# A router's products in four quarters of a bank, and three of eight tiles normalised on VectorE

## The reference, cut to what matters

```
xn = layernorm(x)                      # mean and variance over 256
scores = (xn @ router_w.T + router_b) / max(temperature, 0.1)     # 8192 x 8
gates = sinkhorn(scores)               # 3 rounds of logsumexp, then top 2
s = attention(xn);  ffn = xn + experts(xn, top 2)
out = x + s * silu(ffn)
```

## Time and profile before

| | |
|---|---|
| median of three runs | 1550.58 us |
| the profiled execution | 1555.48 us, span 1553.7 us |
| TensorE busy | 1497.1 us, 96% of the span |
| TensorE idle before L1109 for ScalarE's L864, first 140 us | 11.5 us in 4 waits |
| ScalarE idle before L852 for TensorE's L1109, first 140 us | 10.4 us in 20 waits |
| granted clock, 30 to 36.8 us | 0.50 |

### The profile page before, as it was taken

The page is one execution under the profiler, slowest core; times in us unless marked ns, Lnnn a source line. Parts: engine busy times, 40 slices in busy tenths (PEclk is TensorE's granted clock), DMA queues, the critical chain, the costliest instruction groups (busy, mean ns, idle before and its releaser), DMA issues.

```text
span 1553.7 us, 31511 instructions
## 1 busy us (share of the span) xinstructions
PE 1497.1 (96%) x11036; PEld 1175.4 (76%) x11036; DVE 916.5 (59%) x1730; ACT 788.9 (51%) x1269; POOL 750.6 (48%) x881
## 2 busy tenths in 40 slices
PE   5999799989999999999999999999999999999997
PEld 2546665758888888888888888788887878778775
DVE  7567889954444444444444444466765666576567
ACT  4767334413333333333333333566767776676674
POOL 4504188913666665444444444235365364734365
PEclk9999999989999999999999999999999999999999
DMA  9946432266474746242422351233576555556654
GB/s 324 392 162 216 173 137 72 75 215 228 158 247 158 242 156 241 75 165 77 157 76 89 133 213 56 92 135 123 189 244 218 181 188 179 187 193 202 218 178 136
DMA packets 181330, 267.93 MB, mean 172 GB/s; under 512 B 15944, under 2 KB 123264, under 8 KB 180800
## 3 DMA queue, kind: packets, MB, share of 16 engines
q1 hardware_dynamic: 149920, 196.79, 37.1%
q0 software_dynamic: 12960, 35.41, 6.9%
q10 hardware_dynamic: 18304, 33.72, 6.1%
HBM read 157.97 MB, written 107.89 MB: 171 GB/s over the span
## 4 chain that ended last, share of the span: by engine, by line
PE 83%; DVE 7%; ACT 4%; DMA 3%; issue 2%; SPq 1%; ACTq 0%; DVEq 0%
PE ps L1377 24%; PE ps L1300 18%; PE ps L1396 12%; PE ps L1319 8%; PE ps L1242 5%; PE ps L1386 4%; PE ps L1315 2%; PE ps L1359 2%; ACT WM L964 2%; PE ps L1191 2%; PE ps L1263 2%; PE ps L1119 1%; DMA u_d<-UN 1%; PE ps L1109 1%; DVE UN L1462 1%
## 5 line engine op out<-in xcount | busy, mean ns | idle before, releaser
L1377 PE MATMUL ps<-WR,FR 128*128 x1620 | 405.6, 400 | 1.9 <-DMA WR<-w_d 1.9
L1377 PEld LDWEIGHTS ps<-WR,FR 128*128 128x128 f32 x1620 | 296.2, 190 | 57.0 <-issue 2.1
L775 POOL DMA_INDIRECT y_d<-AUX x135 | 133.6, 990 | 297.0 <-DVE AUX L1943 295.5
L964 ACT ACTIVATE WM<-ps,bcs,trig 128x512 f32<-128x512 f32 x256 | 242.2, 1014 | 63.7 <-PE ps L1300 59.6
L1960 DVE TENSOR_TENSOR AUX<-AUX,ps 128x512 f32<-128x512 f32 x135 | 92.9, 688 | 304.7 <-ACT AUX L1011 304.7
L1011 ACT ACTIVATE AUX<-ps 128x512 f32<-128x512 f32 x135 | 80.6, 597 | 291.2 <-PE ps L1377 291.2
L1870 DVE TENSOR_SCALAR WM<-ps,vec,trig 128x512 f32<-128x512 f32 x208 | 196.6, 1031 | 46.8 <-ACT WM L964 46.6
L1300 PE MATMUL ps<-XH,WH 128*128 128x512 f32 x512 | 208.1, 407 | 7.8 <-issue 4.0
L1396 PE MATMUL ps<-WR,ABR 128*128 x540 | 207.1, 418 | 0.0
L1300 PE MATMUL ps<-XH,WL 128*128 128x512 f32 x512 | 200.6, 392 | 0.0
L1300 PE MATMUL ps<-XL,WH 128*128 128x512 f32 x512 | 200.6, 392 | 0.0
(11 more groups left out here) (268 smaller groups left out, 2497.7 us busy)
## 6 DMA issues: line engine op xcount, KB each, us to landing
US<-u_d SPq DMA_DIRECT2D x62, 512.0 KB, 4.7
u_d<-UN SPq DMA_DIRECT2D x120, 256.0 KB, 2.4
WR<-w_d SPq DMA_DIRECT2D x96, 256.0 KB
AUX<-y_d SPq DMA_DIRECT2D x32, 512.0 KB, 6.4
w_d<-WR ACTq DMA_DIRECT2D x24, 512.0 KB, 3.4
WM<-in_L_attn_x_dram SPq DMA_DIRECT2D x16, 512.0 KB, 9.6
xn_d<-WM SPq DMA_DIRECT2D x32, 256.0 KB, 6.2
mhl_d<-UNR ACTq DMA_DIRECT2D x16, 512.0 KB, 3.1
```

Of the source, the lines that this page charges most:

```text
L775: e.indirect_dma_start(y_d, bass.IndirectOffsetOnAxis(toks[:, n:n + 1], 0), YS[n % 4], None).then_inc(s_y[n % 4], 16)
L964: e.activation(rotated(q, 2 * x, i), b, ACT.Identity, bias=bcs[:, x, 0, i:i + 1], scale=trig[:, 0, i:i + 1]).then_inc(s_ca, 1)
L1377: mm = e.matmul(b[:, :], x, WR[:, bass.ds(off[m] + (2048 * z + 1024 * a + 512 * k), 512)], start=(k == 0 and x is xh and z == 0), stop=(k ...
```

## The change

The products of four pairs now follow each other as one block of eight, first the four with k = 0 into the four quarters, then the four with k = 1. The block of foursome g is issued after the transposes of pair 4g + 5 (the last one at the end). ScalarE's copies go to six buffers instead of two; four of these share their space with `XH` and `XL`, so ScalarE's first copy to `XH` waits for the last block. Tiles 1, 3 and 7 of each eight are normalised on VectorE instead of 3 and 7.

```
-        RT = AB
+        RT = [AB[:, 0, :], AB[:, 1, :], RTX[:, 0, :], RTX[:, 1, :], RTX[:, 2, :], RTX[:, 3, :]]
...
+        ON_DVE = (1, 3, 7)
...
             def routed(i):
                 e.wait_ge(s_rt, i + 1)
-                if i >= 2:
-                    e.wait_ge(s_rm, i - 1)
-                e.activation(RT[:, i % 2, 0:512], (bT, bH)[i % 2][:, :], ACT.Copy).then_inc(s_rtc, 1)
+                if i >= 6:
+                    e.wait_ge(s_rm, 4 * ((i - 6) // 4 + 1))
+                e.activation(RT[i % 6], (bT, bH)[i % 2][:, :], ACT.Copy).then_inc(s_rtc, 1)
...
-                for n in (2 * i, 2 * i + 1)[:2 - i % 2]:
-                    e.activation(X[:, n, :], X[:, n, :], ACT.Identity, bias=nmr[:, n:n + 1],
-                                 scale=rstd[:, n:n + 1]).then_inc(s_xn, 1)
+                for n in (2 * i, 2 * i + 1):
+                    if n % 8 not in ON_DVE:
+                        e.activation(X[:, n, :], X[:, n, :], ACT.Identity, bias=nmr[:, n:n + 1],
+                                     scale=rstd[:, n:n + 1]).then_inc(s_xn, 1)
...
+                else:
+                    e.wait_ge(s_rm, NT // 2)
                 e.activation(XH[:, k, :], pXT[:, :], ACT.Copy).then_inc(s_xtc, 1)
...
-            def rmm(i):
-                e.wait_ge(s_rtc, i + 1)
-                g, a = i // 4, 32 * (i % 4)
-                if a == 0 and g >= 4:
+            def rmm(g):
+                e.wait_ge(s_rtc, 4 * g + 4)
+                if g >= 4:
                     e.wait_ge(s_re, g - 3)
                 for k in range(2):
-                    mm = e.matmul(ps[g % 4][a:a + 32, 0:256], rwT[:, k, :], RT[:, i % 2, 256 * k:256 * k + 256],
-                                  start=(k == 0), stop=(k == 1))
-                mm.then_inc(s_rm, 1)
+                    for a in range(4):
+                        mm = e.matmul(ps[g % 4][32 * a:32 * a + 32, 0:256], rwT[:, k, :],
+                                      RT[(4 * g + a) % 6][:, 256 * k:256 * k + 256], start=(k == 0), stop=(k == 1))
+                mm.then_inc(s_rm, 4)
...
-            for i in range(NT // 2 + 1):
-                if i < NT // 2:
-                    rt(i)
-                if i == 1:
+            for i in range(NT // 2):
+                rt(i)
+                if i == 5:
                     e.wait_ge(s_rwl, 2)
-                if i >= 1:
-                    rmm(i - 1)
+                if i >= 5 and i % 4 == 1:
+                    rmm(i // 4 - 1)
                 if i >= 10 and i % 4 == 2:
                     back(i // 4 - 2)
+            rmm(7)
...
-                for n in range(a + 3, b, 4):
+                for n in (n for n in range(a, b) if n % 8 in ON_DVE):
```

More of the change, by code:

```diff
@@ L88, in program @@
         XB = sb("XB", [128, 4, D])
-        XH = sb("XH", [128, 2, 512], F32R)
-        XL = sb("XL", [128, 2, 512], F32R)
+        with nc.sbuf_tensor("XHL", [128, 4, 512], F32R) as XHL:
+            pass
+        RTX = sb("RTX", [128, 4, 512])
+        XH, XL = XHL[:, 0:2, :], XHL[:, 2:4, :]
         with nc.sbuf_tensor("XHJ", [128, 2, 4, 128], F32R) as XHJ:
@@ L312, in program, with on_act @@
                     firsts.setdefault(slots[k - 3], []).append(j // 4)
+        ON_DVE = (1, 3, 7)
+        def on_act(n):
+            return sum(i % 8 not in ON_DVE for i in range(n))
         host = {QE + 1 + 2 * k: k for k in range(QE)}
@@ L443, in _ @@
                 if q < NQ:
-                    e.wait_ge(s_xn, 3 * q + 3)
-                    e.wait_ge(s_xv, q + 1)
+                    e.wait_ge(s_xn, on_act(4 * q + 4))
+                    e.wait_ge(s_xv, 4 * q + 4 - on_act(4 * q + 4))
                     for a in range(2):
@@ L1103, in rt @@
                     e.wait_ge(s_rtc, i - 1)
-                e.wait_ge(s_xn, 2 * i + 2 - (i + 1) // 2)
-                if i % 2:
-                    e.wait_ge(s_xv, (i + 1) // 2)
+                e.wait_ge(s_xn, on_act(2 * i + 2))
+                if 2 * i + 2 > on_act(2 * i + 2):
+                    e.wait_ge(s_xv, 2 * i + 2 - on_act(2 * i + 2))
                 for n in range(2):
```

## The result

| | median, us | times | ratio to before, 95% interval |
|---|---|---|---|
| before | 1554.15 (1549.31 to 1560.92) | 20 | |
| changed | 1549.51 (1544.45 to 1555.44) | 20 | 0.9968 [0.9955, 0.998] |

The change makes the kernel 0.32% faster, 0.20 to 0.45%. In time that is 4.6 us where 7.5 were forecast. The time, 1549.51, lies outside the range of 1540.5 to 1548.5. One part of this needs no explanation by the kernel: the median of before, over 20 times, is 3.6 above the 1550.58 of the three shown, from which the forecast was subtracted. Taken from 1554.15 the forecast would be 1546.6, and the range 1544.1 to 1552.1, which holds the time measured. So the range was missed by the number that the forecast started from; the gain itself is 2.9 smaller than forecast, and by the interval of the ratio it is 3.1 to 7.0 us.

What follows compares the result with a forecast made beforehand. TensorE was taken to bound the router, 6.50 us a foursome. An earlier last root (3.9) plus a shorter way to the router's end (5.35), less 1.7 for the clock, gave 7.5: 1550.58 to 1543.1 us, range 1540.5 to 1548.5.

Steps and rivals of the forecast that it cites:

- everything else behind the router is released by the router: Behind the router: apart from the attention's weight loads, nothing waits on an absolute time, so the 7.5 us gain survives.
- The block costs 0.98: Router products on TensorE: a block of sixteen records overlaps over four quarters and takes 0.98 us, as one pair's did.
- The third rival: Router products: quarters don't overlap, a block takes 3.9 us, a foursome 7.5 instead of 6.5; 1555 us; chance 0.06.
- ScalarE becomes the bound at 0.49 for each instruction: Router: ScalarE's 9 instructions, 4.4 us a foursome, exceed TensorE's 3.56, so at most 2.1 of 6.50 is won.
- Roots at 42.3 and 53.1: ScalarE's roots of tiles 32-47 and 48-63 in the router, against 43.11 and 57.00; the last is 3.9 us earlier.
- The second rival: VectorE reaches the router's roots later than counted, beside GpSimd, by 2 to 3 us; gain 4.5 to 5.5; chance 0.13.
- From the last root to the router's end 14.0: ScalarE's 23 instructions of 0.49 behind the last root, then 2.49: 14.0 us instead of 19.35, 5.35 less.
- 1.7 for the clock: Half clock on TensorE for some 6.8 us behind a 3.3 us gap before pair 22 takes 1.7 us off the gain.
- The first rival: TensorE stays at half clock through the whole router, a foursome takes 6.2 us, gain some 2, 1548.5 us; chance 0.12.
- Every later stage earlier by the same: Sign in the new profile: stages behind the router move as much as its end, from 76.35 to 68.8 us.
- outside the stage as far as I see: The profiled execution is 4.9 us slower than the median shown for reasons outside the router; 7.5 is subtracted from both.
- The weight loads: Attention's weights behind the router land at 86 us, wanted by VectorE at 92; they cost nothing unless the gain exceeds 13.

Runs made afterwards that it cites:

- the clock kept up: Changed kernel plus dummy transposes of the identity before pairs 8, 15 and 22 (30, 16 and 18) in TensorE's idle time; 1552.71 us, 0.9998 of before.
- the hold: GpSimd's first late split held back until VectorE has split the attention's weights, in the changed kernel (0.9954 of before) and in that with later roots (0.9925, again 0.9942).
- no collision: Changed kernel with GpSimd's first late split held back until VectorE has split the attention's weights; 1548.71 us, 0.9954 of before.
- the best version: Changed kernel with its last two roots right ahead of their tiles and GpSimd's first late split held back; 1546.13 us (0.9925 of before), again 1546.31 (0.9942).
- before with its clock kept up: Kernel before plus 22 dummy transposes of the identity before pair 8, in TensorE's idle time; 1553.47 us, 0.999 of before.
- the late roots' version: Changed kernel with ScalarE's roots of tiles 32-47 and 48-63 moved right ahead of their tiles; 1547.45 us, 0.9954 of before.

## Why the prediction was wrong, point by point

Three steps failed: the sum was made against one execution with a late last root and taken for the median (point 6), the half clock behind the last root was priced too high (point 4), and "everything else behind the router is released by the router" doesn't hold (point 5).

1. **The block costs 0.98: right.** 1.00 on the chain, 1.86 at half clock. The third rival (no overlap, 3.9) is dead.
2. **ScalarE becomes the bound at 0.49 for each instruction: right**, behind the last root.
3. **Roots at 42.3 and 53.1: right within 0.6**, 41.78 and 53.48. The second rival (VectorE late) didn't come: in the mean of the five profiles the last root is at 53.2. That this is so near is in part luck: the six small instructions begin at 51.8 in the mean, not at 51.2, and take 1.45 (0.91 to 2.05), not 1.9.
4. **From the last root to the router's end 14.0: near. 1.7 for the clock: mis-sized.** The trace has 14.94 (68.42 - 53.48), the mean of five 15.05, where the forecast had 15.7. With the clock kept up behind the root it is 14.37 (67.17 - 52.80), by one profile, so the half clock costs some 0.7 there and not 1.7. It did follow the gap ahead of pair 22 (2.64 us long, not 3.3), but lasted 3.4 us and not 6.8. The stretch from 44.8 to 48.2 wasn't foreseen, and what it costs wasn't separated. The first rival (half clock throughout) is refuted by the windows at 1.00.

The Trainium skill (TensorE: Matmul & The Clock Gate, PE-mode transpose), weighed there, says that transposes don't count as busy time for the gate in the same way. The runs say otherwise: with 22 dummy transposes and nothing else added, before had full clock from 30 to 36.8, where the earlier trace rows had 0.50 and another profile of it 0.74 and 0.76. That is full clock kept; whether transposes alone would bring it back from half, no run here shows.

5. **Every later stage earlier by the same: wrong.** This is the step "everything else behind the router is released by the router". GpSimd's splits are released by weight loads, and VectorE's instructions moved onto them. In the mean 0.75 of the 6.7 went there; 0.5 of it is shown by the hold, the 0.25 ahead of Wv x Wo is read from rows alone. In the changed kernel's first profile

```profile
66.71 2.79 POOL L723 TENSOR_TENSOR WL<-WM,WH 128x256 fp32r<-128x256 f32 x4
...
68.88 0.90 DVE L1576 TENSOR_SCALAR AUX<-AUX,tmp_b 128x512 f32<-128x512 f32 x1
```

and in its fourth, where the split is nearly over, 3.55 instead of 3.96 follow the router's end:

```profile
66.98 2.80 POOL L723 TENSOR_TENSOR WL<-WM,WH 128x256 fp32r<-128x256 f32 x4
...
69.57 0.49 DVE L1576 TENSOR_SCALAR AUX<-AUX,tmp_b 128x512 f32<-128x512 f32 x1
```

6. **The sum was made against one execution, and that was an unlucky one.** The prediction saw that it was 4.9 above the median shown and put that "outside the stage as far as I see". 1.4 of it (76.35 - 74.96) were in the stage. Some 0.5 are the six small instructions ahead of the last root, counted at 1.9 for both kernels from the execution in which they met GpSimd; in three of five executions of before they take 0.9 to 1.0. The other 0.9 are their later start in that execution, whose cause is open. So the saving from 57.00 to 53.1, 3.9, is one against a root that stands at 55.6 in the mean (57.00, 54.66, 54.26, 56.56, 55.55): 2.5, and 2.4 with the changed kernel's measured mean. The cheaper half clock, less 0.4 by which 14.0 was short, gave 0.65 back (4.30 behind the root in the mean, where 5.35 - 1.7 = 3.65 was forecast), and so the stage gained 6.7 and not 7.5.

Together: 7.5 forecast, 6.7 in the router's means, less 0.75 given back, 5.9 for the start of the projections. The timed medians show 4.6 (0.9968, interval 3.1 to 7.0) and 6.1 (0.9961 x 1555), so 5.9 agrees with both, and 7.5 lies outside the first. The profiles alone show less: the stretch from the projections' start to TensorE's last instruction is 2.4 longer in the changed kernel's five profiles than in before's, with standard deviations of 1.7 and 1.6. It stays open whether that is real. Against it: "no collision" took 1432.2, the best version 1438.8 and 1433.5 with the same code, and before with its clock kept up 1436.2, though nothing was edited there; so single profiles scatter by about as much as the question is. For it: of the seven profiles of the changed kernel's variants five lie at 1436 or more. One piece can be named: in the first profile of the changed kernel ScalarE waits 11.5 for the landing of u_d, 2.8 more than in before's. The other four don't have it (7.6 to 9.3).

The weight loads held as said: VectorE splits the attention's first weights without a wait for them in the changed kernel,

```profile
92.10 0.68 DVE L1508 CAST WH<-WM 128x1024 fp32r<-128x1024 f32 x1
```

7.5 earlier than in the earlier trace rows.

## What to carry to other kernels

Before a stage's gain is taken over to the whole, look for engines behind it whose times are set by transfers: they stay where they are, and the work that moves falls onto them. Take a stage's time from several profiles; a loop in which small instructions just meet or just miss another engine's long ones can have two times, 1 us apart here. And where an engine is idle ahead of an instruction that others stand behind, move work ahead of it: two changed numbers (the roots) put the router's end 1.7 to 2.8 earlier in three profiles (65.50, 66.56, 65.51 against a mean of 68.27), where the change itself brought 6.7.

## What the runs showed of the hardware

- Sixteen records of 32 weight columns and 256 moving columns take 1.00 us in four quarters of a bank (1.02 with the loops exchanged), the first of each quarter within 0.04 of each other; 1.86 at half clock.
- VectorE's instruction of 128 x 16 lasts 0.17 alone and 0.73 at 26.19 in the earlier trace rows, beside GpSimd; one of 64 x 64 0.25 and 0.94.
- Between executions of one kernel the half clock begins at other times (30.0, 32.0, 31.6, 32.6, 32.3 in before) and lasts 3.4 or 6.8 us, with the same work ahead of it; the fastest profile with 3.4 us of it ends its router at 73.60, the one at full clock at 73.55.
- In the late roots' version 3.4 us at half clock behind the last root go with 1.4 us more to the router's end (13.94 against 12.55 and 12.57).
